# Attention probabilities transposed in 32x32 blocks by VectorE and sixteen DMAs, instead of by TensorE

## What is computed

```
q, k, v = x @ wq.T, x @ wk.T, x @ wv.T          # 32, 8 and 8 heads of 128
s = einsum("bhgnd,bhmd->bhgnm", q, k) * scale   # 64 x 64 scores of each sequence and head
p = softmax(mask(s), axis=-1)
o = einsum("bhgnm,bhmd->bhgnd", p, v)
x = layernorm(x + o @ wo.T)
```

## Time and profile before

| | |
|---|---|
| median of 3 executions | 2420.19 us (2417.53 to 2421.94) |
| the profiled execution | 2417.93 us |
| its span, first to last instruction | 2416.1 us |
| mean granted TensorE clock | 0.971 |
| busy, share of the span | PE 97%, weight loads 78%, DVE 48%, ACT 32%, POOL 31% |
| DMA | 51427 packets, 102.09 MB, engines busy 12.8% |

### The profile page before, as it was taken

The page is one execution under the profiler, slowest core; times in us unless marked ns, Lnnn a source line. Parts: engine busy times, 40 slices in busy tenths (PEclk is TensorE's granted clock), DMA queues, the critical chain, the costliest instruction groups (busy, mean ns, idle before and its releaser), DMA issues.

```text
span 2416.1 us, 34601 instructions
## 1 busy us (share of the span) xinstructions
PE 2332.2 (97%) x12594; PEld 1878.0 (78%) x12594; DVE 1149.3 (48%) x1956; ACT 779.5 (32%) x1475; POOL 753.2 (31%) x709
## 2 busy tenths in 40 slices
PE   8999999997999989998999999999899999999999
PEld 6888888875555557886788888887788888888877
DVE  3444434447677633434444444445345444544456
ACT  2222222223677731222322222322132233223321
POOL 4122122202343335444222222211443333333233
PEclk9999999998999999999999999999899999999989
DMA  3111111000000123211111111110111011101000
GB/s 142 44 40 35 39 43 43 26 28 9 18 14 16 64 70 122 104 52 54 45 45 28 36 39 44 36 32 1 58 44 36 23 35 39 39 17 35 27 32 36
DMA packets 51427, 102.09 MB, mean 42 GB/s; under 512 B 8593, under 2 KB 11153, under 8 KB 50833
## 3 DMA queue, kind: packets, MB, share of 16 engines
q1 hardware_dynamic: 51344, 100.97, 12.8%
HBM read 98.85 MB, written 2.10 MB: 42 GB/s over the span
## 4 chain that ended last, share of the span: by engine, by line
PE 86%; issue 6%; DVE 3%; POOL 3%; ACT 1%; DMA 1%; SPq 0%; POOLq 0%; DVEq 0%; ACTq 0%
PE banks L261 20%; PE banks L263 19%; PE banks L262 19%; PE banks L532 7%; PE banks L585 4%; PE banks L1171 2%; PE banks L1155 2%; PE banks L544 2%; PE banks L572 2%; PE banks L1137 1%; POOL f_wl L1582 1%; PE banks L1144 1%; PE banks L1107 1%; PE banks L1123 1%; POOL f_il L1590 1%
## 5 line engine op out<-in xcount | busy, mean ns | idle before, releaser
L261 PE MATMUL banks<-xTh,wh 128*128 128x512 f32 x1024 | 421.4, 412 | 9.0 <-DVE xTl L1858 7.4
L263 PE MATMUL banks<-xTh,wl 128*128 128x512 f32 x1024 | 405.6, 396 | 0.0
L262 PE MATMUL banks<-xTl,wh 128*128 128x512 f32 x1024 | 404.1, 395 | 0.0
L261 PE MATMUL banks<-woh,oth 128*128 128x512 f32 x768 | 317.9, 414 | 1.0 <-DVE X L848 0.7
L848 DVE TENSOR_TENSOR X<-banks,X 128x512 f32<-128x512 f32 x192 | 132.6, 691 | 381.1 <-PE banks L263 381.1
L262 PE MATMUL banks<-wol,oth 128*128 128x512 f32 x768 | 306.1, 399 | 0.0
L263 PE MATMUL banks<-woh,otl 128*128 128x512 f32 x768 | 305.0, 397 | 0.0
L929 POOL TENSOR_TENSOR sc_sb<-sc_sb,rs 128x512 f32<-128x512 f32 x96 | 100.0, 1046 | 654.0 <-DVE rs L815 654.0
L672 ACT ACTIVATE q_sb<-banks 128x512 f32<-128x512 f32 x192 | 114.5, 596 | 420.4 <-PE banks L263 420.4
L261 PEld LDWEIGHTS banks<-xTh,wh 128*128 128x128 f32 x1024 | 195.8, 191 | 49.4 <-issue 9.2
L263 PEld LDWEIGHTS banks<-xTh,wl 128*128 128x128 f32 x1024 | 194.9, 190 | 44.9
(11 more groups left out here) (209 smaller groups left out, 4041.6 us busy)
## 6 DMA issues: line engine op xcount, KB each, us to landing
raw<-in_a_in SPq DMA_DIRECT2D x144, 256.0 KB, 2.7
raw<-in_a_out SPq DMA_DIRECT2D x96, 256.0 KB, 2.6
f_q<-in_f_q SPq DMA_DIRECT2D x21, 512.0 KB, 4.2
f_s<-in_f_s SPq DMA_DIRECT2D x21, 512.0 KB, 5.2
X<-in_x SPq DMA_DIRECT2D x1, 2048.0 KB, 10.5
x_craw<-in_ctx SPq DMA_DIRECT2D x8, 256.0 KB, 2.6
x_ct<-in_ctxT_pair SPq DMA_DIRECT2D x16, 128.0 KB, 2.0
f_c<-in_ctxT SPq DMA_DIRECT2D x2, 1024.0 KB, 5.2
```

The lines of the kernel that those rows point to most:

```text
L261: nc.tensor.matmul(out, w_hi, x_hi, start=start, stop=False)
L262: nc.tensor.matmul(out, w_hi, x_lo, start=False, stop=False)
L263: return nc.tensor.matmul(out, w_lo, x_hi, start=False, stop=stop)
```

## The change

The transposes leave PE. A new event TR stands in the list ahead of the PT of the same couple: DVE transposes every 32x32 block of the couple's 128x512 tile of probabilities, in one instruction, into a new tile `pq`. That leaves each block in its old group of 32 partitions. SP then issues sixteen DMAs of 32 partitions x 512 bytes (`move_probs`), which carry every block to the partitions where it belongs, in a new tile `pt`; both tiles have two buffers. ACT and DVE read `pt` in SBUF for `pth` and `ptl`, where they read PSUM before. The columns of `pt` are in another order, so the moving operand of the PV matmuls is read with a pattern in runs of 32 elements. TR0 and TR1 come in the couple's own iteration, TR2 and TR3 in the next one. Six of the events around them change places: PT0 moves ahead of U_1 in all three stages, and in the tail PV0 moves to the front, ahead of WO6, with PT1 and TR3 ahead of WO7 and PT2 behind WO0. `move_probs` of couples 2 and 3 stands between the loads `load_w` 1 and 2 and behind `load_w` 3, that of couples 0 and 1 between the loads `load_o`. At the end of a stage two more `move_probs` follow the last load.

```diff
     if rms:
-        ev = events("U_0 U_1 PT0- WS0- WS1- U_2 PV0- PT1- WS2- WS3- U_3 WO0- PV1- U_4 KT0 PT2- WO1- U_5 KT1 PV2- WO2- SQ0 "
-                    "U_6 PT3- U_7 WO3- SQ1 PV3- SC0 WO4- SC1 U_8 U_9 WO5- SQ2 U_10 U_11 WO6- SQ3 SC2 WO7- SC3")
+        ev = events("U_0 PT0- TR2- U_1 WS0- WS1- U_2 PV0- PT1- TR3- WS2- WS3- U_3 WO0- PV1- U_4 KT0 PT2- WO1- U_5 KT1 PV2- WO2- SQ0 "
+                    "U_6 PT3- U_7 WO3- SQ1 PV3- SC0 WO4- SC1 U_8 U_9 WO5- SQ2 TR0 U_10 U_11 TR1 WO6- SQ3 SC2 WO7- SC3")
     else:
-        ev = events("U_0 VT1- U_1 PT0- WS0- WS1- U_2 PV0- PT1- WS2- WS3- U_3 WO0- PV1- U_4 PT2- WO1- U_5 PV2- WO2- SC0 "
-                    "PT3- WO3- SC1 U_6 PV3- WO4- U_7 WO5- U_8 WO6- U_9 WO7- SC2 U_10 SC3 U_11 VT0")
+        ev = events("U_0 VT1- PT0- TR2- U_1 WS0- WS1- U_2 PV0- PT1- TR3- WS2- WS3- U_3 WO0- PV1- U_4 PT2- WO1- U_5 PV2- WO2- SC0 "
+                    "PT3- WO3- SC1 U_6 PV3- WO4- U_7 WO5- U_8 TR0 WO6- U_9 TR1 WO7- SC2 U_10 SC3 U_11 VT0")
     if not project:
-        return events("WO6-- " + ("" if rms else "VT1- ") + "PT0- WO7-- WS0- WS1- PV0- PT1- WS2- WS3- PV1- PT2- WO0- WO1- "
+        return events("PT0- TR2- PV0- WO6-- " + ("" if rms else "VT1- ") + "PT1- TR3- WO7-- WS0- WS1- PV1- WS2- WS3- WO0- PT2- WO1- "
                       "PV2- WO2- PT3- WO3- PV3- WO4- WO5- WO6- WO7-")
...
+            def move_probs(i, pair):
+                st.need(sp, "t_done", 4 * i + pair + 1)
+                for q in range(4):
+                    for bk in range(4):
+                        sp.dma_start(pt[32 * bk:32 * bk + 32, pair % 2, q * P:(q + 1) * P],
+                                     pq[32 * q:32 * q + 32, pair % 2, bk * P:(bk + 1) * P]).then_inc(pt_in[pair % 2], 16)
...
-            def step(i, more):
-
-                if more:
-                    for c in range(5):
+            def step(i, before, more):
+
+                first, second = (1, 2) if st.rms else (0, 1)
+                for c in range(5):
+                    if more:
...
+                    if before and c in (1, 3):
+                        move_probs(i - 1, 2 + c // 2)
                 for c in range(4):
...
                     load_o(i, c, c)
+                    if c in (first, second):
+                        move_probs(i, c - first)
...
-            step(NKV - 1, False)
+            step(NKV - 1, True, False)
+            for pair in (2, 3):
+                move_probs(NKV - 1, pair)
...
-            def transpose_probs(i, pair):
-                st.need(pe, "p_ready", 4 * i + pair + 1)
-                st.need(pe, "pt_ready", 4 * i + pair)
-                rows = sc_sb[:, pair, :, :].rearrange("p c s -> p (c s)")
-                for t in range(2):
-                    for c in range(2):
-                        last = nc.tensor.transpose(pb[4][:, (2 * t + c) * P:(2 * t + c + 1) * P],
-                                                   rows[:, (2 * c + t) * P:(2 * c + t + 1) * P], ident[:, :])
-                last.then_inc(A["t_done"], 1)
...
+                by_query = [p[:, :].rearrange("p (a c t i) -> p t c a i", a=4, c=2, t=2) for p in (pth, ptl)]
...
-                        st.need(act, "t_done", 4 * j + n + 1)
-                        nc.scalar.activation(pth[:, :], pb[4][:, :], ACT.Copy).then_inc(A["pt_hi"], 1)
+                        pt_wait(act, st, j, n, 1)
+                        st.need(act, "pv_done", 4 * j + n)
+                        nc.scalar.activation(pth[:, :], pt[:, n % 2, :], ACT.Copy).then_inc(A["pt_hi"], 1)
...
+            def transpose_probs(i, pair):
+
+                st.need(dve, "p_ready", 4 * i + pair + 1)
+                pt_wait(dve, st, i, pair, 0)
+                nc.vector.transpose(pq[:, pair % 2, :].rearrange("p (bk ct i) -> p ct bk i", bk=4, i=32),
+                                    sc_sb[:, pair, :, :].rearrange("p c s -> p (c s)").rearrange(
+                                        "p (ct bk i) -> p ct bk i", bk=4, i=32)).then_inc(A["t_done"], 1)
...
-                        nc.vector.tensor_tensor(ptl[:, :], pb[4][:, :], f32(pth[:, :]),
+                        nc.vector.tensor_tensor(ptl[:, :], pt[:, n % 2, :], f32(pth[:, :]),
                                                 ALU.subtract).then_inc(A["pt_ready"], 1)
```

More of the change, by code:

```diff
@@ L164, in program @@
             kfac = sb("kfac", [P, 1])
+            pq = sb("pq", [P, 2, 512])
+            pt = sb("pt", [P, 2, 512])
         with ExitStack() as sx:
@@ L307, in program @@
         ld_b = sem("ld_b")
+        pt_in = [sem(f"pt_in{n}") for n in range(2)]
         xs = {n: sem("x_" + n) for n in (
@@ L413, in spread_rows, with pt_wait @@
             return col.rearrange("p (c o) -> p c o", o=1).to_broadcast([P, 8, S])
+        def pt_wait(eng, st, i, pair, more):
+            wait(eng, pt_in[pair % 2], 256 * (16 * st.index + 2 * i + pair // 2 + more))
         def input_quarter(n):
@@ L490, in step @@
                     load_w(i + 1, 5, 4)
-            step(0, True)
+            step(0, False, True)
             with sp.Fori(1, NKV - 1) as i:
-                step(i, True)
-            step(NKV - 1, False)
+                step(i, True, True)
+            step(NKV - 1, True, False)
+            for pair in (2, 3):
+                move_probs(NKV - 1, pair)
         def pe_attention(pe, st):
@@ L579, in probs_v @@
                 st.need(pe, "o_ready", 8 * i + 2 * pair)
+                by_query = [p[:, :].rearrange("p (a c t i) -> p t c a i", a=4, c=2, t=2) for p in (pth, ptl)]
                 for t in range(2):
                     cols = slice(t * G * S, (t + 1) * G * S)
-                    for v_part, p_part in ((vh, pth), (vh, ptl), (vl, pth)):
+                    for v_part, p_part in ((vh, 0), (vh, 1), (vl, 0)):
                         for b in range(2):
                             r = slice(64 * b, 64 * b + 64)
-                            last = nc.tensor.matmul(PVB[b][:, cols], v_part[r, 2 * pair + t, :], p_part[r, cols],
-                                                    start=v_part is vh and p_part is pth, stop=v_part is vl)
+                            last = nc.tensor.matmul(PVB[b][:, cols], v_part[r, 2 * pair + t, :], by_query[p_part][r, t],
+                                                    start=v_part is vh and p_part == 0, stop=v_part is vl)
                 last.then_inc(A["pv_done"], 1)
@@ L615, in run @@
                         transpose_v(j, n)
-                    elif kind == "PT":
-                        transpose_probs(j, n)
                     elif kind == "PV":
@@ L833, in run @@
                         sums(j, n)
+                    elif kind == "TR":
+                        transpose_probs(j, n)
                     elif kind == "PT":
                         st.need(dve, "pt_hi", 4 * j + n + 1)
-                        nc.vector.tensor_tensor(ptl[:, :], pb[4][:, :], f32(pth[:, :]),
+                        nc.vector.tensor_tensor(ptl[:, :], pt[:, n % 2, :], f32(pth[:, :]),
                                                 ALU.subtract).then_inc(A["pt_ready"], 1)
```

## The result

| | median us | runs | span of the profiled execution | granted clock |
|---|---|---|---|---|
| before (same chip) | 2419.1 | 2417.5 to 2421.9 | 2416.1 | 0.971 |
| changed | **2514.3** | 2511.9 to 2521.7 | 2510.1 | 0.957 |

The changed kernel is slower: the ratio is **1.0396**, 95% interval 1.0379 to 1.0412. The forecast was 2440 with a range of 2400 to 2482, so the direction is right and the size is wrong: it named +20 us and the change cost 95.

What follows compares the result with a forecast made beforehand. PE, busy 97% of the span, was taken as the bound. -40 + 6 + 8 + 28 + 15 + 9 = +26 us on the profiled execution's 2417.9 gave 2444, stated as 2440 us, range 2400 to 2482.

Steps and rivals of the forecast that it cites:

- clock, in no segment: PE's granted clock dips after waits in the tails and xattn1: +9 us, bounds -10 and +20.
- price of an issue: SP, each of a couple's 16 DMA issues: 0.47 us, bounds 0.33 and 0.66, so a move holds SP 7.5 us.
- SP becomes the bound of the hand-over: Rival: issues cost 0.58 us, chunk 5 comes late, delaying xattn1's TR2, U_3, WO0: 2474; at 0.66 over 2500; chance 0.14.
- The removed transposes: PE, 96 groups of four transposes gone at 0.42 us each, bounds 0.36 and 0.45: -40 us.
- DVE's transpose: DVE, 96 new transposes of 0.7 us each, bounds 0.4 and 1.4, on a half-idle engine.
- PV's strided operand: PE, PV's operand read in runs of 32 elements: 0 us taken, upper bound 34 us.
- WO0 of attn0 and attn1: Last quarter's weights 0.5 us behind PE's need in each of twelve iterations: +6 us.
- WO0 of xattn1: PE waits 3.3 us for otl in each of six iterations, +20; the first, with chunk 5 late, 8: +28 us.
- The first full iterations: attn0 and attn1: TR2 at 12.7 us instead of 5, WO0 done 3.9 us late, two stages: +8 us.
- The tails: Stage ends: PE waits at PV0, SP busy with moves 2 and 3, later loads late: +15 us, bounds 5 and 25.

Runs made afterwards that it cites:

- via_dram: The changed kernel with a couple's 16 moves replaced by one write to device memory and four reads back; 2402.3 us, ratio 0.9926.
- via_dram_16: via_dram with its four reads of 64 KB a couple cut into sixteen of 16 KB; 2510.3 us, ratio 1.0397.
- w5_then_bias: The changed kernel with SP issuing the next head's chunk 5, then the moves of couples 0 and 1, then the next bias; 2465.7 us, ratio 1.0177.
- via_dram_late: via_dram with xattn1's U_1 back ahead of PT0 and DVE's transposes of couples 2 and 3 behind the PV0 and PV1 splits; 2402.1 us.

## Why the forecast was wrong, by its steps

The times of DVE's addition of WO7 to `X` cut each trace into nine segments. The table gives how much longer each is than in the kernel before, the forecast's terms with their share of the transposes (about), and the kernel with 12 moves, which has the forecast's price of a move.

| segment | forecast | changed | 12 moves | via_dram |
|---|---|---|---|---|
| to attn0's first full iteration | +2 | +8.9 | +1.9 | +1.1 |
| attn0, 5 iterations | -6 | +0.2 | -7.6 | -7.4 |
| attn0's last and tail | +2 | +13.6 | +3.0 | +1.7 |
| xattn0, ffn0, to attn1's first | +2 | +9.3 | +4.4 | +0.2 |
| attn1, 5 iterations | -6 | +6.3 | -7.6 | -7.4 |
| attn1's last and tail | 0 | +5.2 | -1.3 | -0.2 |
| to xattn1's first | +6 | +5.0 | +1.6 | -0.5 |
| xattn1, 5 iterations | +8 | +26.6 | +2.5 | -4.5 |
| last head, tail and gate | +7 | +18.9 | +5.7 | +2.0 |
| clock, in no segment | +9 | | | |
| sum | +24 | +94.0 | +2.6 | -15.0 |

(The forecast's own sum is +26; the two are rounding and the first half iteration.)

- **The step that failed is the price of an issue.** "Back to back, issues follow each other at 534.69 - 534.21 = 0.48 us ... I take 0.47": those were issues that read device memory, and for them it is right (0.46 in via_dram_16). The moves read on-chip memory and take 0.63. The forecast had 0.66 as its upper bound, and its rival "SP becomes the bound of the hand-over" said "at 0.66 over 2500" with the mechanism seen here: chunk 5 late, TR2 late, U_3 and WO0 with it. It gave that 0.14. The row that should have weighed more was the bias load's 0.58, in pieces of 256 B and in the same kernel.
- **That one term is worth 92 us**, more than the 74 between forecast and result: the rest of the sum was 18 us too high. By the table the 92 us lie in all three stages: 24 in xattn1's five iterations, 22 in those of attn0 and attn1, and 46 in the starts and tails. The wait for the key/value units' bank stood in the rival alone and not in the sum. With SP held as the forecast had it, by 12 moves in place of 16, the forecast's column and the measured one agree within 2 us in six of nine segments.
- *The removed transposes*: 0.37 a group measured, 0.42 taken. Inside the bounds; the sum had 5 us too many saved.
- *DVE's transpose*: 0.705 us (median), 0.7 taken, and PV's strided operand costs next to nothing: its second and third matmuls take 279 ns each in attn0 of via_dram against 278 and 275, its first 333 against 328. Right.
- *WO0 of attn0 and attn1*, 0.5 us an iteration on `wol`: with SP in time, in via_dram, there is no such wait (0.43 us once and 0.15 us once). Wrong by 6 us.
- *WO0 of xattn1*: 2.65 us against 3.3, the mechanism as forecast. But by the medians of via_dram and via_dram_late it costs nothing net; the forecast added +28 for it and +9 for the clock. Those two are most of why 12 moves came to 2422 and not to the forecast's 2440.
- *The first full iterations*: 3.9 us late was forecast; with 12 moves PE waits 2.7 and 5.1 us, in the changed kernel 8.3 and 10.5.
- *The tails*: with the moves at 10 us SP is held 20.4 us by moves 2 and 3 of the last head, and what waits for its next loads is late by as much. Of the kernel's end, SP, POOL and PE:

```profile
2414.39 20.38 SPq L459 DMA_DIRECT2D pt<-pq  x32
2434.87 0.52 SPq L1663 DMA_DIRECT2D g_raw<-in_g_gate  x1
...
2438.00 0.65 POOL L1679 TENSOR_SCALAR g_h<-g_raw 128x552 fp32r<-128x552 f32 x1 [24.95 <-DMA g_raw<-in_g_gate]
...
2443.47 0.47 PE L352 MATMUL banks<-ident,X 128*128 128x128 f32 x1 [9.01 <-DVE X L344]
```

  This is the forecast's own mechanism, PE waiting for the normalised X behind the splits of `g_raw`, now with 9.0 us.
- *Which way the clock goes.* By the mean granted clock of the two pages, (1 - 0.957) x 2510 = 108 us of the changed span were missing at full speed, and 70 of the one before: up to 38 us of the 94, if PE had worked through all of them. With 12 moves it is 68. In the changed kernel the low clocks stand where PE waits longest (0.90 and 0.87 in xattn1's last head and the tail behind it), so I count them as a part of the price of the late chunk; that is argued and not shown.

Not tried: why an issue takes longer when it reads on-chip memory, and why chunk 5 lands later behind moves. In attn0 of the changed kernel that is 3.1 to 3.6 us after its issue, and 4.8 in the iteration shown, against 2.4 to 2.7 in the kernel before and 2.6 to 2.8 in w5_then_bias, where it goes ahead of the moves of couples 0 and 1.

## What to carry to other kernels

Count what a rearrangement by DMA costs its issuing queue before what it costs the DMA engines: 16 issues of 16 KB held SP for 10 us while each landed in 1.8. Then ask for the most urgent transfer that stands behind them in that queue, who splits it, and who stands behind the splitter; the cost was small here until that chain reached the bound engine, and then 2.5 us more of hold a couple cost 92 us. Fewer, larger transfers with the rearrangement in the address pattern, or the urgent load ahead, turn the same idea from 4% slower to 1.3% faster.

## What was not expected of the hardware

- An issue of 32 rows of 512 B costs SP 0.63 us when the source is on-chip memory and 0.46 when it is device memory (10.02 and 7.29 us for sixteen); ACT pays 0.61. The source is not the only thing that counts: two bias loads in pieces of 256 B, from device memory, take 1.31 us. A round trip by device memory, five transfers with a wait for the first to land in between, held SP 4.8 us in the median and never over 6.2.
- With a regular wait of 2.65 us in each xattn1 iteration the granted clock was 1.00 in 25 of 30 iterations and 0.92 in five; without it, it was 1.00 in three of ten and 0.94 to 0.98 in seven. The whole kernels took the same time (2402.3 and 2402.1 us, 2388.9 and 2389.0). To take an idle stretch away from a TensorE that is busy for 96% of an iteration need not shorten the kernel.
